# Transposing the masks of a key lookup by DMA from SP's queue in place of TensorE and ScalarE, with a new slot table

## The reference

```
x = x + mamba(layernorm(x))        # block a: conv, silu, a scan over time with 256 x 16 states, feed-forward, layernorm
x = x + experts(layernorm(x))      # experts 1
x = x + block_b(layernorm(x))      # gated scan over time with 16 states, tanh, projection, layernorm
x = x + experts(layernorm(x))      # experts 2, same weights
```

```
q = (x @ w_q).reshape(b, n, 2, HEADS, DIM_KEY)
sim = einsum(q, keys)                         # 2 x 8 groups of 32 similarities
scores, best = the best sum of one entry of each of the two groups
index = key1 * 32 + key2                      # one of 8192 experts per head
h = gelu(dot(x, w_down[index])) * relu(score)
out = sum over heads of h * w_up[index]
```

## Time and profile before

| | us |
|---|---|
| median of 3 runs | 2204.65 (2204.11 to 2206.53) |
| the profiled execution | 2206.03 |
| its span, first to last instruction | 2204.3 |
| DVE busy | 1805.9 (82%) |
| PE busy | 1638.3 (74%) |
| POOL busy | 1538.0 (70%) |
| ACT busy | 1496.9 (68%) |
| PE transposes of masks, L679, 512 of them | 45.8 |
| ACT copies of them, L965, 64 of them | 65.2 |

### The profile page before, as it was taken

The page is one execution under the profiler, slowest core; times in us unless marked ns, Lnnn a source line. Parts: engine busy times, 40 slices in busy tenths (PEclk is TensorE's granted clock), DMA queues, the critical chain, the costliest instruction groups (busy, mean ns, idle before and its releaser), DMA issues.

```text
span 2204.3 us, 24242 instructions
## 1 busy us (share of the span) xinstructions
PE 1638.3 (74%) x6099; PEld 908.3 (41%) x6186; DVE 1805.9 (82%) x4265; ACT 1496.9 (68%) x3199; POOL 1538.0 (70%) x1147
## 2 busy tenths in 40 slices
PE   5677586878787978787887878787878777856533
PEld 2233243434444544344544445444445444434322
DVE  1989697889998989999899989899999999743221
ACT  3555575857786867878677868777777776546532
POOL 1023636288888888888888888888888888767344
PEclk8899898989999989999999999999999998967766
DMA  2001111022323222232222232222323222333212
GB/s 53 10 0 34 53 30 57 24 70 72 89 67 89 70 81 74 72 84 71 84 67 84 72 87 68 82 71 72 86 69 85 67 82 73 97 93 108 58 53 81
DMA packets 79898, 151.03 MB, mean 69 GB/s; under 512 B 20584, under 2 KB 46592, under 8 KB 79680
## 3 DMA queue, kind: packets, MB, share of 16 engines
q0 software_dynamic: 49152, 134.28, 21.3%
q1 hardware_dynamic: 29344, 14.65, 2.4%
q10 hardware_dynamic: 1248, 0.34, 0.1%
HBM read 145.01 MB, written 4.19 MB: 68 GB/s over the span
## 4 chain that ended last, share of the span: by engine, by line
DVE 37%; issue 20%; PE 18%; POOL 12%; ACT 10%; another core or an unknown queue 1%; DMA 1%; DVEq 1%; ACTq 0%; POOLq 0%
DVE hp L1321 12%; POOL rows L1429 10%; DVE rows L1244 7%; PE bank L709 5%; DVE hp L1330 4%; DVE hp L1311 4%; ACT rows L984 3%; PE bank L668 3%; PE ysum L768 3%; DVE top L1211 2%; ACT flip L965 1%; DVE st L1182 1%; DVE mask L1218 1%; ACT L914 1%
## 5 line engine op out<-in xcount | busy, mean ns | idle before, releaser
L1429 POOL DMA_INDIRECT rows<-in_experts,index x1024 | 1302.7, 1272 | 360.7 <-issue 297.8
L1321 DVE TENSOR_TENSOR_SCAN hp<-dA,hp 128x1024 f32<-128x1024 f32 x256 | 617.9, 2414 | 10.5 <-ACT dA L1005 8.5
L768 PE MATMUL ysum<-hp,ident 128*128 128x512 f32 x1024 | 504.1, 619 | 18.5 <-POOL hp L1444 16.4
L1005 ACT ACTIVATE dA<-delta,decay 128x511 f32<-128x511 f32 x512 | 334.1, 710 | 46.8 <-POOL delta L1459 19.3
L1244 DVE CUSTOM_DVE_ANT_0 rows<-rows,xn 128x128 f32<-128x128 f32 x1024 | 272.2, 328 | 97.1 <-DMA rows<-in_experts,index 97.0
L984 ACT ACTIVATE rows<-rows,coef 128x128 f32<-128x128 f32 x1024 | 308.8, 390 | 39.4 <-DVE coef L1251 39.4
L1311 DVE TENSOR_TENSOR hp<-du,bcast 128x1024 f32<-128x1024 f32 x256 | 307.1, 1199 | 22.6 <-POOL du L1463 15.6
L751 PE MATMUL bcast<-split,pick 128*128 128x512 bf16 x438 | 154.1, 397 | 188.1 <-DVE hp L1311 175.9
L768 PEld LDWEIGHTS ysum<-hp,ident 128*128 128x128 f32 x1024 | 201.5, 198 | 185.0 <-issue 139.8
L1444 POOL TENSOR_TENSOR hp<-hp,c_row 128x1024 f32<-128x1024 f32 x48 | 115.3, 2403 | 231.0 <-ACT c_row L1022 230.6
L709 PE MATMUL bank<-rows,ident 128*128 128x256 f32 x1024 | 248.6, 399 | 35.4 <-ACT rows L984 35.4
(11 more groups left out here) (179 smaller groups left out, 2190.2 us busy)
## 6 DMA issues: line engine op xcount, KB each, us to landing
rows<-in_experts,index POOLq DMA_INDIRECT x1024, 2.8
x_in<-in_x SPq DMA_DIRECT2D x16, 256.0 KB, 3.9
x_res<-in_x SPq DMA_DIRECT2D x16, 256.0 KB, 4.4
y<-x SPq DMA_DIRECT2D x16, 256.0 KB, 2.7
rows<-in_taps SPq DMA_DIRECT2D x1, 512.0 KB
rows<-in_wq_t SPq DMA_DIRECT2D x1, 512.0 KB, 5.5
rows<-in_in_proj_t ACTq DMA_DIRECT2D x1, 256.0 KB
rows<-in_key_t SPq DMA_DIRECT2D x1, 128.0 KB, 5.5
```

What stands on the lines that cost most here:

```text
L768: mm = nc.tensor.matmul(ysum[:, j, :], ident[:], hp[:, BUFFER[k], j, :], start=(k == 0), stop=(k == NS - 1))
L1005: op = nc.scalar.activation(dA[:, n % NDA, j, 1:T], delta[q][:, j, 1:T], ACT.Exp, scale=decay[:, j, n:n + 1])
L1321: nc.vector.tensor_tensor_scan(flat, dA[:, n % NDA, :, :].rearrange("p a b -> p (a b)"), flat, 0.0, ALU.mult, ALU.add).then_inc(scanned, 1)
L1429: pool.indirect_dma_start(e.rows[:, t, h, :], None, A["experts"], bass.IndirectOffsetOnAxis(ap=e.index[:, t, h:h + 1], axis=0)).then_inc(e ...
```

## The change

`experts_flip` goes from PE and from ACT. SP gets a function in its place, which issues eight DMA transposes per half, from `mask` to `flip`, both in SBUF. `experts_code` on PE waits for all eight of its half, and DVE's `experts_top` waits for them before it overwrites the mask. The bank of PSUM is not claimed for the flip any more. Both slot tables are new throughout.

```diff
+FLIPS = 16 * HALF * (SIM // P)
 ...
         @block.sync
         def _(sp):
+            def flip(e, n, half):
+
+                sp.wait_ge(e.masked, at(n, NT, (half + 1) * HALF - 1))
+                sp.sem_inc(e.opened_flip, 1)
+                if half == 1:
+                    sp.wait_ge(e.coded, at(n, 2, 0))
+                elif later(n):
+                    sp.wait_ge(e.coded, at(n - 1, 2, 1))
+                sp.sem_inc(e.opened_flip, 1)
+                for t in range(HALF):
+                    for c in range(SIM // P):
+                        chunk = slice(c * P, (c + 1) * P)
+                        sp.dma_start_transpose(e.flip[:, t, chunk], e.mask[:, t, chunk]).then_inc(e.flipped, 16)
+
 ...
+                    for m, r, k in due("sp_flip_e2", i, q, slot):
+                        flip(e2, m, k)
+                    for m, r, k in due("sp_flip_e1", i, q, slot):
+                        flip(e1, m, k)
                     for m, r, _ in due("sp_store", i, q, slot):
 ...
             def experts_code(e, k, i, m, stage, half):
 
                 claim(k, i)
-                pe.wait_ge(e.flipped_sb, at(m, 2, half))
+                pe.wait_ge(e.flipped, at(m, 2, half) * FLIPS)
 ...
                 if half == 1:
-                    dve.wait_ge(e.flipped, at(n, 2, 0))
+                    dve.wait_ge(e.flipped, at(n, 2, 0) * FLIPS)
                 elif later(n):
-                    dve.wait_ge(e.flipped, at(n - 1, 2, 1))
+                    dve.wait_ge(e.flipped, at(n - 1, 2, 1) * FLIPS)
```

The slots around the lookup in the steady part (all in phase POST), and a few others that the prediction speaks of:

```diff
-    "pe_sim_e1": (POST, (30, 35, 43, 45)),
-    "pe_flip_e1": (POST, (40, 49)),
-    "pe_code_e1": (POST, (40, 50)),
+    "pe_sim_e1": (POST, (30, 37, 42, 44)),
+    "pe_code_e1": (POST, (41, 51)),
-    "act_flip_e1": (POST, (43, 49)),
+    "sp_flip_e1": (POST, (41, 44)),
-    "dve_top_e1": (POST, (36, 43, 47, 50)),
-    "dve_index_e1": (POST, (44, 54)),
+    "dve_top_e1": (POST, (37, 42, 46, 49)),
+    "dve_index_e1": (POST, (45, 53)),
-    "pe_sim_e2": (POST, (175, 177, 182, 183)),
-    "pe_flip_e2": (POST, (179, 185)),
-    "pe_code_e2": (POST, (181, 190)),
+    "pe_sim_e2": (POST, (175, 178, 182, 183)),
+    "pe_code_e2": (POST, (181, 192)),
-    "act_flip_e2": (POST, (180, 190)),
+    "sp_flip_e2": (POST, (189, 198)),
-    "dve_top_e2": (POST, (179, 180, 185, 187)),
+    "dve_top_e2": (POST, (179, 180, 185, 186)),
     "dve_index_e2": (POST, (184, 194)),
-    "dve_dot_e2": (POST, (227, 233, 234, 238)),
-    "dve_weigh_e2": (POST, (243, 245)),
+    "dve_dot_e2": (POST, (227, 233, 235, 239)),
+    "dve_weigh_e2": (POST, (244, 247)),
-    "act_out_e2": (POST, (250, 252)),
+    "act_out_e2": (POST, (255, 255)),
-    "pool_fetch_e1": (POST, (56, 58, 63, 66)),
-    "pool_fetch_e2": (POST, (205, 222, 223, 234)),
+    "pool_fetch_e1": (POST, (46, 52, 63, 65)),
+    "pool_fetch_e2": (POST, (218, 221, 224, 228)),
-    "sp_xres": (POST, (26,)),
-    "sp_store": (POST, (220,)),
+    "sp_xres": (POST, (34,)),
+    "sp_store": (POST, (255,)),
 ...
```

More of the change, by code:

```diff
@@ L153 @@
     "pe_ff2": (POST, (0,)),
[L154 to L167, removed]
@@ L196 @@
[L196 to L208, removed]
@@ new lines @@
+    "pe_xp": (POST, (116,)),
+    "pe_gate": (POST, (117,)),
+    "pe_y": (POST, (123,)),
+    "pe_z": (POST, (132,)),
+    "pe_ln_c": (POST, (135,)),
+    "pe_turn_e2": (POST, (166,)),
+    "pe_sim_e2": (POST, (173, 177, 182, 184)),
+    "pe_code_e2": (POST, (178, 187)),
+    "pe_sum_e2": (POST, (241, 250)),
+    "act_out": (POST, (0,)),
+    "act_gelu": (POST, (1,)),
+    "act_rstd_a": (POST, (2,)),
+    "act_rstd_e1": (POST, (4,)),
+    "act_norm_e1": (POST, (7,)),
+    "act_turn_e1": (POST, (25,)),
@@ L670, in experts_sim @@
                 fill(k, i, m, stage, t, e.masked, NT, t)
-            def experts_flip(e, k, i, m, stage, half):
-                claim(k, i)
-                pe.wait_ge(e.masked, at(m, NT, (half + 1) * HALF - 1))
-                flat = bank[k][:].bitcast(BF16)
-                for t in range(HALF):
-                    for c in range(SIM // P):
-                        mm = nc.tensor.transpose(flat[:, t * SIM + c * P:t * SIM + (c + 1) * P],
-                                                 e.mask[:, t, c * P:(c + 1) * P], ident16[:])
-                mm.then_inc(e.flipped, 1)
-                fill(k, i, m, stage, half, e.flipped_sb, 2, half)
             def experts_code(e, k, i, m, stage, half):
                 claim(k, i)
-                pe.wait_ge(e.flipped_sb, at(m, 2, half))
+                pe.wait_ge(e.flipped, at(m, 2, half) * FLIPS)
                 for t in range(HALF):
@@ L777, in iteration @@
                         experts_sim(e2, 0, i, m, "pe_sim_e2", k)
-                    for m, r, k in due("pe_flip_e2", i, q, slot):
-                        experts_flip(e2, 0, i, m, "pe_flip_e2", k)
                     for m, r, k in due("pe_code_e2", i, q, slot):
@@ L864, in iteration @@
                         experts_sim(e1, 1, i, m, "pe_sim_e1", k)
-                    for m, r, k in due("pe_flip_e1", i, q, slot):
-                        experts_flip(e1, 1, i, m, "pe_flip_e1", k)
                     for m, r, k in due("pe_code_e1", i, q, slot):
@@ L957, in experts_turned @@
                 nc.scalar.activation(e.xnT[:], bank[k][:], ACT.Copy).then_inc(e.turned_sb, 1)
-            def experts_flip(e, k, m, half):
-                act.wait_ge(e.flipped, at(m, 2, half))
-                if half == 1:
-                    act.wait_ge(e.coded, at(m, 2, 0))
-                elif later(m):
-                    act.wait_ge(e.coded, at(m - 1, 2, 1))
-                nc.scalar.activation(e.flip[:].rearrange("p t g -> p (t g)"), bank[k][:].bitcast(BF16),
-                                     ACT.Copy).then_inc(e.flipped_sb, 1)
             def experts_gelu(e, m, half):
@@ L1047, in iteration @@
                         nc.scalar.activation(xnbT[:], bank[2][:], ACT.Tanh, bias=b_d[:, 0:1]).then_inc(b_y_sb, 1)
-                    for m, r, k in due("act_flip_e1", i, q, slot):
-                        experts_flip(e1, 1, m, k)
                     for m, r, k in due("act_gelu_e1", i, q, slot):
@@ L1164, in iteration @@
                         experts_turned(e2, 0, m)
-                    for m, r, k in due("act_flip_e2", i, q, slot):
-                        experts_flip(e2, 0, m, k)
                     for m, r, k in due("act_gelu_e2", i, q, slot):
```

191 lines of the change are left out of this document (101 added, 90 removed).

## The result

| | before | after |
|---|---|---|
| median of the runs made together, us | 2205.59 | 2491.70 (2488.89 to 2493.20, 4 runs) |
| ratio, 95% interval | | 1.1295 [1.1281, 1.1308] |
| span of the profiled execution | 2204.3 | 2489.8 |

The kernel is 13% slower. The direction was forecast, the size was not: 2305 was the time, 2470 the upper end, and what came is the rival of slow transposes (2511).

The account below looks back on a forecast made before the run. DVE was taken to set the pace, idling 7 to 8 us per turn. From 2206 us, +98 stalls, +17 tail and -15 relief gave 2306, less 1.4 for the profiled run: 2305 us, 4.5% slower; range 2183 to 2470.

Parts of the forecast that it names:

- the rival of slow transposes: Rival for SP's transposing DMAs: each holds the queue as long as a gather holds POOL, L 12.8, 2511 us; chance 0.24.
- What goes: PE transposes and ACT copies removed: relief of 1 us per turn (0 to 4.1), -15 us over 15 turns.
- What comes: Eight transposing DMAs per half on SP, which PE's code matmul awaits: 8.1 us against 2.4 from mask to code before.
- L: Time from a half's second mask to the landing of its eighth transpose: 8.1 us, from 5.4 to 12.8.
- the other bound: Upper bound of L, from POOL's gather at 1.25 us per instruction and 2.8 to landing: 12.8 us.
- The sign of being wrong: On SP: issue pitch under 0.5 us (turn near 120), or over 1.1 us (turn past 135).
- What DVE does meanwhile: DVE's stalls before its index instructions: 3.5, 1.3 and 2.0 us at three halves, zero at the fourth; 98 us.
- The covers: DVE's work between second mask and index: 5.1 and 7.3 us for experts 1, 5.3 and 16.6 for experts 2.
- PE's queue: Work behind PE's waiting code matmul: next similarity, second `pe_dt`, two spreads and a state's sum; nothing added.
- SP's queue: Store of y and load of x ahead of the last flip, which starts some 5.2 us after the mask; stall zero.
- The tail: Last batches, with nothing to hide behind: three halves times 8.1 - 2.4, 17 us longer (9 to 31).
- The point of decision: L of about 6.5, at which the faster rival (2190 us, chance 0.23) is decided.

Follow-up runs that it names:

- e1: Changed kernel with transposes issued only for the very first half of each experts block, later halves reusing that flip; 2164.72 us, ratio 0.9815 to the kernel before.
- e13: Changed kernel with the slot table of before and transposes only for the very first half of each experts block; 2219.29 us, ratio 1.0054 to the kernel before.
- e7: Changed kernel with one transposing DMA per token tile (512 columns), two per half instead of eight; 2167.91 us, ratio 0.9816 to the kernel before.
- e10: Changed kernel with one transposing DMA per half (1024 columns) instead of eight; ratio 0.9747 to the kernel before.
- e14: Changed kernel with PE's first sum of experts 2 one slot later, behind the similarity; 2490.52 us, ratio 1.1295 to the kernel before.
- e4: Changed kernel with SP's second load of x moved ahead of the flips, slot 34 to 2; 2477.06 us, ratio 1.1227 to the kernel before.
- e2: Changed kernel with only four of the eight transposes of each half issued; 2244.47 us, ratio 1.0173 to the kernel before.

## Why the prediction was wrong

**What goes.** I took 1 us per turn, 15 us, from a range of 0 to 4.1. With the new table it is 120.7 - 117.5 = 3.2 us per turn and 41 us in all (`e1`); with the old it is none (`e13`). The bounds held, the value was low, and the reason given was wrong: relief was to help "only where DVE waits for a late ACT or PE", but DVE waited as long as before, and its own instructions took 42.7 us less. I had priced the table at zero, and without it there is no gain. ACT's busy time fell by 53.6 us (65 forecast). PE's rose by 56 instead of falling by 46. Windows of the kernel after, the first over a turn's length, the second a wait at the code:

```profile
1250.00:1375.00 125.00, 91.77 (x314) 51.31 (x318) 94.07 (x237) 77.22 (x169) 82.38 (x65) 0.85 0.27 75
...
1264.50:1275.00 10.50, 2.00 (x5) 0.57 (x3) 5.03 (x19) 2.38 (x5) 8.24 (x6) 0.76 0.39 100
```

The mean granted clock is 0.85 where it was 0.96, a mixture with more of the lower of its two levels (1.2 and 2.4 GHz), and 0.76 where PE is busy 2.00 of 10.5 us. The sums of states took 655 ns each (L771) against 619 before (L768).

**What comes: the step that failed.** "The nearest row by kind is SP's load of the padded w_xproj ... I take L = 8 x 0.72 + 2.3 = 8.1 us." The landing was right, 2.33 us; the pitch was 1.27 us and L 11.5. A DMA in short pieces is near to a transposing one in its bytes, but it is not the same instruction, and the row that came out near was the other bound, POOL's gather at 1.25 us; that these two agree is chance as far as any run shows. The sign of being wrong that I had named came: a pitch over 1.1 us and a turn over 135 (140.3).

VectorE: DVE Perf Modes of the Trainium skill, The three transpose paths, gives 1309 ns for a 128x128 bf16 block through the DMA. The 1.27 us from one issue to the next agree with it, and the widened instructions of `e7` and `e10` show that at these sizes it is a price of each instruction and not of each block. Advanced Engine Details and Errata of the Trainium skill, X-Bar Transpose, calls transposing DMAs on trn2 as fast as regular ones. In issue, which decides here, that doesn't hold: they take 1.23 us against 0.39.

**What DVE does meanwhile.** The covers were nearly right. With L = 11.5 the steps of the prediction give stalls of 12.05 - 5.1 = 6.95, 12.05 - 7.3 = 4.75 and, with SP free 4.1 us late (8 x 1.27 - 6.1) and the second stall as cover, 12.05 + 4.1 - 5.3 - 4.75 = 6.1. The turn shown has 6.83, 3.21 (with 1.28 at a similarity ahead) and 4.62; the third is smaller since the second mask came 7.5 us after that of the half before it and not 6.1, so that SP was only 2.7 us late. The second half of experts 2 costs nothing, as forecast: 28 waits in nine turns are three per turn. The formula gives 15 x 11.7 + 13 x 6.1 = 255 us, 17.8 per turn; measured are 15.0 per turn.

**PE's queue.** "DVE needs the spread issued there only one or two states later (feed 13 in slot 49), so I add nothing". The next similarity stood in my list and got no price: it was this that DVE then needed, and PE reached it late by its stand at the code: 4.4 us more per turn. `e14` shows the wait moving with the order and not going.

**SP's queue.** I had put the store ahead of the flip and not the second load of x behind it. By `e4` having it there costs 14.6 us: small, since POOL had slack, as forecast for the gathers.

**The tail.** 17 us were forecast; three halves times 11.5 - 2.4 give 27, and the span grew by 29.8 us behind the twelfth store. That is near by luck. SP's queue after the twelfth store of after:

```profile
2222.16 78.66 SPq L616 DMA_TRANSPOSE flip<-mask  x32
...
2343.53 36.46 SPq L616 DMA_TRANSPOSE flip<-mask  x16
...
2417.74 29.83 SPq L616 DMA_TRANSPOSE flip<-mask  x16
```

With the eight at 2164.29 these are nine halves, and the chain of waits runs through eight of them, not three. Against `e1_once` the transposes cost 51.2 us there, and the new kernel without them is 21.4 us shorter than before in that part (274.9 against 296.3), which I had not forecast.

**The sum.** The pitch is what was mis-sized. It is 0.55 us too small eight times, 4.4 us; the formula counted an eighth gap that isn't there (-1.3) and no start of SP (+0.3), which leaves the 3.4 us between 8.1 and 11.5. By the prediction's own formulas that is 255 - 98 = 157 us in the stalls and 10 in the tail, of the 186 by which the forecast was short: 2472 us.

Of the 20 us that are left I can't say that any one term holds them, for the others don't cancel by themselves. The relief came out 26 us larger, PE's queue costs some 57 (4.4 x 13, an estimate) and the load of x 15, which would overshoot by 26; the stalls were smaller than the formula has them, and the tail larger. The slow rival's 2511 is near in the same way: its L of 12.8 was 1.3 us too long, and it had neither queue in it.

Nine turns of before and eight of after, from store to store (700.45 to 1789.00 and 761.42 to 1884.16), give the turn as DVE spent it. Its idle time grew from 7.9 to 29.6 us per turn: 14.4 of that growth at the code, 4.4 at similarities, 1.8 at gathers, and 1.1 in small pieces (the parts by the lists of waits, the whole by busy times). Its busy time fell from 113.1 to 110.8. Together that is the 19.4 us by which these turns are longer.

The point of decision, L about 6.5, fits: `e2` with 6.8 is 1.7% slower, `e7` with 5.7 is 1.8% faster. The 3 us of relief per turn that it rests on came too, but not from fewer waits.

## What to carry to other kernels

A transfer that replaces on-chip work is priced by the time from the last producer to the last landing, and where several are issued in a row that is the issue pitch times their number: measure the pitch of that very kind of DMA, and put many pieces in one instruction before judging the idea. Only what exceeds the cover counts, so the first half of a delay can cost a third of the second (80 and 247 us here). Removing work from engines off the bound gave nothing in the old order and 41 us in the new one, and there as shorter instructions of the bound engine, not as fewer waits: compare its busy time as well as its idle time. And an instruction that now waits must be read with all that its queue holds behind it.

## What was not expected of the hardware

A transposing DMA of 128 partitions in bf16 takes SP 1.2 us of issue, for 128, 512 and 1024 columns alike, and those of 128 columns follow each other every 1.27 us; the plain ones shown take 0.37 to 0.67 us. From the start of its issue a 128-column one lands after 2.33 us; of one with 1024 columns the use began after 3.7 us (1011.32 to 1015.04 in `e10`). The 512 small ones took 160 packets each ((111264 - 29344)/512), and yet the DMA engines' share is 0.27 in the 125 us window as before: the engines were far from full, and `e7` moves the same bytes at no cost, so what bounded was the issue.
